# Two attentions in a fused two-layer kernel: the last heads merged without a detour, and another order of score, product and first-pass matmuls in every slot

## What is computed

```python
# layer 0 (4096 given keys) and layer 1 (1024 keys from the same tokens), per head
scores = einsum('bqhd,khd->bhqk', Q, K) * SCALE
attn = softmax(scores, axis=-1)
out = einsum('bhqk,khd->bqhd', attn, V).reshape(B, QL, HIDDEN)
x = x + gate * (out @ Wo.T)          # layer 1 adds a bias as well
```

## Time and profile before

| | us |
|---|---|
| median of three runs (2009.97 to 2014.08) | 2013.04 |
| the profiled execution's own time | 2001.37 |
| its span in the trace | 1999.5 |
| PE busy in the span | 1757.2 |
| DVE busy | 1423.7 |
| ACT busy | 1091.8 |
| POOL busy | 509.8 |

### The profile page before, as it was taken

How to read it: one execution, slowest core, us unless ns; L and a number is a source line. 1 busy time by engine, 2 the same in 40 slices (tenths; PEclk the granted TensorE clock), 3 DMA queues, 4 the chain that set the end, 5 groups by cost and what they waited for, 6 DMA issues and landing times. The chain is left out here.

```text
span 1999.5 us, 28186 instructions
## 1 busy us (share of the span) xinstructions
PE 1757.2 (88%) x9884; PEld 1042.1 (52%) x9884; DVE 1423.7 (71%) x1910; ACT 1091.8 (55%) x2169; POOL 509.8 (25%) x524
## 2 busy tenths in 40 slices
PE   4699999999999999467998664999999999769997
PEld 3233333333333333343343223888888888658885
DVE  4589999999999994565897536666666666556666
ACT  0178888888888885233786412545455445324342
POOL 4333344333454500031213202111011110012223
PEclk8689999999999999676998856999999999879998
DMA  3202111113111100202444101000000000023331
GB/s 121 57 27 59 40 40 50 53 44 95 44 53 52 54 20 24 75 16 44 99 99 132 63 26 33 22 9 21 21 13 21 10 19 3 9 75 110 114 116 59
DMA packets 50127, 102.18 MB, mean 51 GB/s; under 512 B 10279, under 2 KB 20471, under 8 KB 48497
## 3 DMA queue, kind: packets, MB, share of 16 engines
q1 hardware_dynamic: 49745, 100.47, 18.0%
q10 hardware_dynamic: 288, 0.49, 0.2%
HBM read 68.19 MB, written 17.01 MB: 43 GB/s over the span
## 5 line engine op out<-in xcount | busy, mean ns | idle before, releaser
L660 DVE TENSOR_REDUCE a_max_part<-psum 128x1 f32<-128x1024 f32 x640 | 752.6, 1218 | 111.6 <-PE psum L549 109.9
L730 ACT ACTIVATE a_probs<-psum 128x512 f32<-128x512 f32 x1280 | 671.3, 601 | 187.5 <-PE psum L600 186.7
L600 PE MATMUL psum<-a_q_max,a_k_rows 51*128 51x512 f32 x1280 | 467.7, 457 | 7.8 <-ACT a_probs L730 6.0
L600 PEld LDWEIGHTS psum<-a_q_max,a_k_rows 51*128 51x128 f32 x1280 | 214.5, 191 | 369.8 <-ACT a_probs L730 297.3
L549 PE MATMUL psum<-a_k_rows,a_q_rows 48*128 48x512 f32 x1280 | 366.1, 485 | 31.5 <-DVE a_max_part L660 12.4
L589 PE MATMUL psum<-a_probs,a_v_ext 128*32 128x512 f32 x2560 | 353.6, 623 | 1.5 <-ACT a_probs L730 1.5
L549 PEld LDWEIGHTS psum<-a_k_rows,a_q_rows 48*128 48x128 f32 x1280 | 158.4, 194 | 110.3 <-DVE a_max_part L660 85.2
L1687 PE MATMUL psum<-high_t_parts,high_gu 128*128 128x512 f32 x600 | 146.5, 394 | 6.8 <-DVE high_t_parts L1781 6.8
L359 POOL TENSOR_TENSOR a_k_rows<-a_k_in,a_k_rows 16x2048 fp32r<-16x2048 f32 x32 | 146.9, 4592 | 2.5
L483 POOL TENSOR_TENSOR a_max_bf<-a_neg_max,a_zeros 128x8 bf16<-128x8 f32 x64 | 14.5, 227 | 470.7 <-issue 408.2
L1392 PE MATMUL psum<-wide_k_t,wide_q_t 128*128 128x512 f32 (+3 forms) x576 | 130.8, 353 | 1.7 <-DVE wide_id_bf L1591 1.7
(11 more groups left out here) (193 smaller groups left out, 2059.7 us busy)
## 6 DMA issues: line engine op xcount, KB each, us to landing
o<-a_o_out SPq DMA_DIRECT2D x60, 256.0 KB, 2.0
a_k_in<-in_k SPq DMA_DIRECT2D x32, 256.0 KB
a_q_rows<-q_high SPq DMA_DIRECT2D x124, 64.0 KB, 2.4
gu_in<-in_w_gu SPq DMA_DIRECT2D x25, 256.0 KB, 2.9
high_cw<-cw SPq DMA_DIRECT2D x24, 256.0 KB, 3.8
a_k_in<-in_k SPq DMA_DIRECT2D x32, 128.0 KB
a_v_in<-in_v SPq DMA_DIRECT2D x16, 256.0 KB, 12.8
a_o<-o SPq DMA_DIRECT2D x8, 512.0 KB
```

The source lines that it names most:

```text
L600: pe.matmul(psum[:, self.bank_of(self.filling(j)), :], k_rows[rows, b, k0:k0 + P], self.q_max[rows, u % 2, :], start=True, stop=True).then ...
L660: dve.tensor_reduce(self.max_part[:, u % 2, c // self.nch, c % self.nch:c % self.nch + 1], psum[:, 2 * (n % 2):2 * (n % 2) + 2, :], AX.XY, ...
L730: act.activation(self.probs[:, p % self.pring, :], psum[:, self.bank_of(self.filling(j)), :], ACT.Exp).then_inc(self.exp_done, 1)
```

## The change

- **Slot order** (both attentions): two second scores, a pair of first scores, (the turning of maxima), one second score, the products with values, one second score, a pair of first scores.
- **Direct heads.** Heads 14 and 15 both stay on the core (`o_out` has four buffers). A token tile of 128 is one product of `o_out` with `w_direct`: the weights repeated for the four strips, with a column that adds up the denominators. DVE then takes a reciprocal per token and one `scalar_tensor_tensor` adds to x. There are 16 such steps, and four pair steps for the merged heads 0 to 13: 20 in all (`product`, `add_out`). 16 of them lie behind the last ten slots in the first attention, 10 behind the last five in the second (`steps_after`); the others follow the last product with values.
- **Merged heads** have two parts, 0 to 7 and 8 to 13; the second is loaded in two portions. Loads, additions, reciprocals and scaling move to other units, one addition of sums per unit in place of two; the last additions are on POOL, none on DVE.
- **The gate** is multiplied into the weights on POOL (`gate_weights`, unit 11), and the bias's steps come two units later.
- **The first loads of q** of three heads are shared between SP's and ACT's queues.

```diff
-LAST = H - 1
...
-    PARTS = ((0, 8, 0, 0), (8, 12, 1, 0), (12, LAST, 1, 64))
+
+
+    PARTS = ((0, 8, 0), (8, DIRECT[0], 1))
+    STEPS = 20
+    PAIRS = 12
...
+    def load_direct(self, sp, g):
+        if g == 0:
+            sp.wait_ge(self.w_clear, 1)
+        sp.dma_start(self.w_direct[32 * g:32 * g + HD, :, 0:D],
+                     self.w_dram[HD * DIRECT[0]:HD * H, :].rearrange("(h d) n -> d h n", d=HD)).then_inc(self.w_loaded, 16)
...
+    def widen(self, sp, n):
+        lo, hi, c = self.PARTS[n]
+        sp.wait_ge(self.rec_stored[n], 16)
+        if n > 0:
+            sp.wait_ge(self.o_ready[n - 1], 1)
+        sp.dma_start(self.rec_wide[self.rows(n), :],
+                     self.den_dram[lo:hi, :].unsqueeze(1).broadcast_to([hi - lo, HD, T])).then_inc(self.wide_loaded[n], 16)
...
+    def gate_weights(self, pool):
+        gate = self.gate.unsqueeze(1).broadcast_to([P, 2, D])
+        pool.wait_ge(self.w_loaded, 80)
+        pool.tensor_tensor(self.w[:, :, :], self.w[:, :, :], gate, ALU.mult).then_inc(self.w_gated, 1)
+        pool.tensor_tensor(self.w_direct[:, :, 0:D], self.w_direct[:, :, 0:D], gate, ALU.mult).then_inc(self.w_gated, 1)
+        pool.wait_ge(self.w_gated, 2)
...
+    def is_pair(self, k):
+        return self.PAIRS <= k < self.PAIRS + 4
+
+    def tile_of(self, k):
+        return k if k < 8 else k - 8 if k < self.PAIRS else k - self.PAIRS
...
-    def scale_last(self, dve, half):
-        dve.wait_ge(self.last_full, half + 1)
-        for i in range(2):
-            cut, out = slice(256 * i, 256 * (i + 1)), slice(QH * half + 256 * i, QH * half + 256 * (i + 1))
-            dve.reciprocal(self.rec_last[:, cut], self.psum[0:HD, 2, cut]).then_inc(self.rec_last_ready, 1)
-            dve.wait_ge(self.rec_last_ready, 2 * half + i + 1)
-            dve.tensor_tensor(self.o_last[:, out], self.psum[0:HD, 3, cut], self.rec_last[:, cut], ALU.mult).then_inc(self.last_done, 1)
...
+        if self.is_pair(k):
+            i = k - self.PAIRS
+            dve.wait_ge(self.out_free, 8 + 2 * i + 2 if i < 2 else 2 * i + 2)
+            dve.tensor_tensor(self.x[:, 2 * i:2 * i + 2, :], self.x[:, 2 * i:2 * i + 2, :],
+                              self.psum[:, bank, :].rearrange("p (a n) -> p a n", n=D), ALU.add).then_inc(self.out_free, 1)
+            return
+        t = self.tile_of(k)
+        dve.reciprocal(self.rec_token[:, k:k + 1], self.psum[:, bank, D:D + 1]).then_inc(self.token_ready, 1)
+        dve.wait_ge(self.token_ready, k + 1 - (4 if k >= self.PAIRS else 0))
+        if k >= 8:
+            dve.wait_ge(self.out_free, t + 1 if k < self.PAIRS else self.PAIRS + t // 2 + 1)
+        dve.scalar_tensor_tensor(self.x[:, t, :], self.psum[:, bank, 0:D], self.rec_token[:, k:k + 1], self.x[:, t, :],
+                                 ALU.mult, ALU.add).then_inc(self.out_free, 1)
...
-    def select_last(self, pe, half):
-        pe.wait_ge(self.o_full, 2 * LAST + half + 1)
...
+        if k >= 4:
+            pe.wait_ge(self.out_free, k - 3)
+        if self.is_pair(k):
+            i = k - self.PAIRS
+            if i == 0:
+                for ready in self.o_ready:
+                    pe.wait_ge(ready, 1)
+            deep = self.rows(1)
+            for a in range(2):
+                token, out = slice((2 * i + a) * P, (2 * i + a + 1) * P), self.psum[:, bank, a * D:(a + 1) * D]
+                pe.matmul(out, self.o[:, 0, token], self.w[:, 0, :], start=(a == 0), stop=False)
+                mm = pe.matmul(out, self.o[deep, 1, token], self.w[deep, 1, :], start=False, stop=(a == 1))
+            mm.then_inc(self.out_full, 1)
+            return
+        t, n = self.tile_of(k), int(k >= 8)
+        pe.wait_ge(self.o_full, 2 * DIRECT[n] + t // 4 + 1)
+        pe.matmul(self.psum[:, bank, 0:D + 1], self.o_out[:, 2 * n + t // 4, (t % 4) * P:(t % 4 + 1) * P], self.w_direct[:, n, :],
+                  start=True, stop=True).then_inc(self.out_full, 1)
...
+    def steps_after(self, u, g):
+        if self.groups >= 8:
+            s = (u - 2 * DIRECT[1]) * self.groups + g - 6
+            if 0 <= s < 6:
+                return range(2 * s, 2 * s + 2)
+            return range(s + 6, s + 7) if 6 <= s < 10 else range(0)
+        s = (u - 2 * DIRECT[1]) * self.groups + g + 1
+        return range(2 * s, 2 * s + 2) if 0 <= s < 5 else range(0)
...
@@ -428,9 +465,8 @@
             sp.wait_ge(self.q_set, 1)
             if not raw:
                 sp.wait_ge(self.k_set, 1)
-            load_q(sp, (0,), q_rows[:, 0, :], k_rows[:, 0, :], 0, self.q_loaded[0])
-            for h in range(1, first_heads):
-                load_q(sp, (0, 1), q_rows[:, h, :], k_rows[:, h, :], h, self.q_loaded[h])
+            for h in range(first_heads):
+                load_q(sp, (0,), q_rows[:, h, :], k_rows[:, h, :], h, self.q_loaded[h])
             got = first_heads
             if raw:
                 sp.wait_ge(self.v_ready, 1)
...
@@ -456,16 +492,23 @@
                     sent += 1
                 if u == 2:
                     merge.load_weights(sp)
+                if 2 <= u < 6:
+                    merge.load_direct(sp, u - 2)
                 if u == 16:
-                    merge.load(sp, 0)
-                if u == 20:
+                    merge.load_den(sp, 0, 0, 8)
+                if u in (18, 20):
+                    merge.load_sums(sp, 0, 0, 8, range(u - 18, u - 16))
+                if u == 23:
+                    merge.store_reciprocals(sp, 0)
+                if u == 24:
                     merge.widen(sp, 0)
-                if u == 24:
-                    merge.load(sp, 1)
-                if u == 27:
-                    merge.widen(sp, 1)
-            merge.load(sp, 2)
-            merge.widen(sp, 2)
+                    merge.load_den(sp, 1, 8, 12)
+                if u == 25:
+                    merge.load_sums(sp, 1, 8, 12, range(4))
+            merge.load_den(sp, 1, 12, 14)
+            merge.load_sums(sp, 1, 12, 14, range(4))
+            merge.store_reciprocals(sp, 1)
+            merge.widen(sp, 1)
         @block.gpsimd
         def _(pool):
...
@@ -507,26 +551,22 @@
                     if raw:
                         self.split_keys(pool, h)
                 done = heads_split(u)
-                if u == 4 and merge.bias is not None:
+                if u == 6 and merge.bias is not None:
                     merge.scale_bias(pool)
-                if u in (6, 7) and merge.bias is not None:
-                    merge.add_bias(pool, u - 6)
-                if u == 18:
+                if u in (8, 9) and merge.bias is not None:
+                    merge.add_bias(pool, u - 8)
+                if u == 11:
+                    merge.gate_weights(pool)
+                if u == 21:
                     merge.add_den(pool, 0)
-                if u == 20:
-                    merge.add_sums(pool, 0, (1, 2))
-                if u == 21:
-                    merge.add_sums(pool, 0, (3,))
-                if u == 23:
+                if 22 <= u < 25:
+                    merge.add_sums(pool, 0, (u - 21,))
+                if u == 26:
                     merge.scale(pool, 0)
-                if u == 25:
+                if u == 29:
                     merge.add_den(pool, 1)
-                if u == 26:
-                    merge.add_sums(pool, 1, (1, 2))
-                if u == 27:
-                    merge.add_sums(pool, 1, (3,))
-                if u == 29:
-                    merge.scale(pool, 1)
+            merge.add_sums(pool, 1, (1, 2, 3))
+            merge.scale(pool, 1)
         @block.tensor
         def _(pe):
...
@@ -605,27 +645,27 @@
                 j = group * g
                 one = u * steps + 2 * g + ahead
                 two = one + 1
-                second_wait(u, j)
-                second_chunk(u, j)
+                for n in (j, j + 1):
+                    second_wait(u, n)
+                    second_chunk(u, n)
                 if one < self.chunks:
                     first_wait(one)
                     first_half(one, 1)
                     first_half(one, 0).then_inc(self.s1_full, 1)
-                second_wait(u, j + 1)
-                second_chunk(u, j + 1)
                 if j + 2 == self.turn_at and u + 1 < us:
                     turn_maxima(u + 1)
+                second_wait(u, j + 2)
+                second_chunk(u, j + 2)
+                if g > 0:
+                    pv_group(u, g - 1)
+                elif u > 0:
+                    pv_group(u - 1, groups - 1)
+                second_wait(u, j + 3)
+                second_chunk(u, j + 3)
                 if two < self.chunks:
                     first_wait(two)
                     first_half(two, 0)
                     first_half(two, 1).then_inc(self.s1_full, 1)
-                for n in (j + 2, j + 3):
-                    second_wait(u, n)
-                    second_chunk(u, n)
-                if g > 0:
-                    pv_group(u, g - 1)
-                elif u > 0:
```

(88 more changed lines are left out.)

118 lines of the change are left out of this document (46 added, 72 removed).

## The result

The changed kernel takes 2060.3 us in the median of four runs (2055.9 to 2062.5), the kernel before 2011.5 (2004.5 to 2014.1): a ratio of 1.0245, with a 95% interval of 1.0214 to 1.0277. The forecast was 2031.5, range 2005 to 2070. The sign was right; the size was 49 us where +18.5 was forecast. The profiled execution has a span of 2060.6 us, against 1999.5. These spans are 61 us apart and the medians only 49, as the profiled execution of the kernel before was 10 us under its median and that of the changed kernel 2 above.

What follows compares the result with a forecast made beforehand. It took the loop through ACT's exponential and the products, 2.605 us a slot, as the bound. Units +37.5, tail -5, second attention's loop +21.9, tail -36.4, gate half a microsecond: +18.5, from 2013.0 to 2031.5 us, range 2005 to 2070.

Steps and rivals of the forecast that it cites:

- The slot's loop stays at 2.605: In plain slots, the loop through ACT's exponential and the products keeps its five terms, 2.605 us; price 0.
- the ring's wait: PE's wait for a free score bank, said to hide a fifth score round of 0.23 us per slot.
- D: Slower: a same-strip weight load can't overlap a running matmul; slots of 2.75, +37 us, 2068 in all; chance 0.04.
- E: Faster: the score ahead of the products finds its bank free; slots of 2.45, -34 us, 1998 in all; chance 0.06.
- Rival B: Faster or even: the second attention's stalls vanish and both tails end well; sum -5, 2005 to 2019 us; chance 0.12.
- The wait once a unit: Slot 1's products wait for DVE's copy: 1.03 us, second attention 1.24; with the turning, +37.5 over the first attention's units.
- t0: The end of the products in slot 0 of a unit, from which the copy's end was timed.
- The turning: The turning of maxima, once a unit, lies wholly on the path: 0.22 us in the first attention, 0.16 in the second.
- The tails: Time behind each attention's last turning of maxima: -5 us in the first attention, -36.4 in the second.
- Stalls in the second attention: Stalls in the second attention's loop, 38 us before: POOL's long waits for sums and denominators go, 11.6 us stay.
- The clock: PE's granted clock falls after long waits in the second attention: 2.2 us per fall, 8 us for three or four.
- Rival C: Much slower: PE's clock falls again and again from a 1.24 us wait every second-attention unit; 2060 to 2140 us; chance 0.12.

Runs made afterwards that it cites:

- copy-early run: The changed kernel, but DVE copies the sums out after the first chunk of a unit, not the second; PE's order untouched: 1962.4 us.
- run with three useless matmuls: The changed kernel with three unneeded repeats of the third score in slot 1 of the second attention's units, ahead of the waiting products: 2030.2 us.
- order alone: The kernel before with the changed kernel's slot order and the old merging: 2104.8 us, ratio 1.0485.
- early loads: The changed kernel with sums of heads 0 to 7 loaded in units 17 and 19, added and scaled a unit later: 2057.8 us.

## Why the forecast was too small

- **The slot's loop stays at 2.605: right.** The products of neighbouring slots in the changed kernel, by the timeline of PE:

```profile
412.78 1.07 PE L629 MATMUL psum<-a_probs,a_v_ext 128*32 128x512 f32 x8
...
415.39 1.06 PE L629 MATMUL psum<-a_probs,a_v_ext 128*32 128x512 f32 x8
...
417.98 1.07 PE L629 MATMUL psum<-a_probs,a_v_ext 128*32 128x512 f32 x8
```

  They are 2.60 apart: the fifth round hides in the ring's wait. Rivals D and E fall with it, no slot of 2.75 and none of 2.45. The Trainium skill, "TensorE: Matmul & The Clock Gate", Part 3, on which D leaned, lets a load run beside a matmul only where the row group differs. By that rule five exposed loads would stand in this slot; the trace disagrees with it here too. Rival B falls as well: it needed the stalls of the second attention to vanish, and 28 us of them are left, as shown below.
- **The wait once a unit: right.** The copy was forecast to be seen at t0 + 2.635; the load starts at t0 + 2.68. The first attention's unit is 22.58 where 22.59 followed, and the term of +37.5 measures +38.8. The copy-early run takes the wait away and leaves PE's order as it is, and the units go to 21.50.
- **The turning: right**, 0.19 and 0.17 in the copy-early run, against 0.22 and 0.16; its slot is 3.27, against 3.255.
- **The tails: right within 2 us**, -3.6 (forecast -5) and -34.7 (forecast -36.4).
- **Stalls in the second attention: too small.** 11.6 us were forecast. The run with three useless matmuls has a loop of 234.8 us, of which 29 units of 7.14 are 207; so 28 us are stalls, with the falls of the clock that they bring along: 11.9 in the one unit of 19.05 (1.9 forecast), 5.1 where POOL waits for the widened reciprocals (3.7 forecast), 4.0 in the last two units (0.3 forecast), 6.8 in the others (5.7 forecast). The step that failed is the sentence that the waits of 9 to 11 us for sums go, since "loads are issued units before POOL needs them". POOL needs all four strips' sums for its first addition. SP issues the last two in its unit 20, once DVE has copied that unit's sums, and POOL comes to its unit 22 early, as it splits the maxima of the unit after. So the two steps are 6 us apart and not two units: issued at 1154.37, awaited from 1160.37, there at 1167.03, 12.7 us after the issue. Nor are POOL's waits for DMAs gone but for one or two. There are five of 30.4 us in all, three of them in the loop (6.66, 7.31 and 5.67), where the kernel before had six of 34.4. The first row was misread as well: its 9.90 us are a wait for DVE's copy. The wait for sums stands elsewhere in that trace:

```profile
1121.40 2.33 POOL L173 TENSOR_TENSOR h_t<-a_o 64x1024 f32<-64x1024 f32 x1 [9.35 <-DMA a_o<-o]
```

- **The clock: the term that failed most.** I allowed 8 us for three or four falls. It was 30.8, the difference between the changed kernel's loop and that of the useless matmuls. A fall costs two units of 7.14 another 2.7 us (7.70 + 9.28 - 14.28); I had 2.2. The size of one was near, the number of them wrong: I tied the fall to a long wait for POOL and took the new wait of 1.24 us in every unit for harmless. The two terms were 19.6 us together and measured 58.5.
- **The sum.** The like of the profiled execution was forecast at 2019.9 and took 2062.5, 42.6 more; these two terms make 38.9 of it. One slip is in the working: with all stalls gone the loop would be 7.1 x 29 = 205.9, which is +2.3 and not +3.5; nothing but rival B's sum hangs on it. The result lies in the range of 2005 to 2070 only because the range was drawn out for C and D; the forecast's own, 2018 to 2046, missed it.
- **Rival C** named this mechanism, with the right point from which it decides, and gave 2060 to 2140; the result lies at its lower end. The fault was to give it 0.12 and to leave it out of the sum. No row of the kernel before showed a wait of about a microsecond that comes back every unit, so nothing in the trace spoke against it. In the first attention C didn't come true: the wait is 1.02 us there, but once in 22.6 us, and the granted clock is 1.00 on the mean of the 679 us; one unit of 24.2 us has a short stretch at the lower level.

What stays open: the order alone has 16 us more in the first attention than the wait explains (two long units and a longer tail) with the old merging. That part wasn't taken apart. Also open is why the second attention's loop, in the new order, is 265.6 us with the new merging and 253.5 with the old one; the early loads take those 12 us from the loop, but the tail gives back 9. And why the two orders differ at a wait of about 1 us is not known.

## What to carry to other kernels

When an edit moves a consumer ahead in one engine's order, move its producer's step on the other engine with it: here one index in DVE's order was worth 98 us. A short wait can have two prices, its own length and what it does to TensorE's clock, and here the second hung on how often it returned: 1.2 us in every 7 cost nearly as much again through the clock (30.8 us over 29 units, beside 36 for the wait itself), 1.0 in every 22.6 hardly more than itself. And of two edits that come in one change, measure each alone: the merging gave 53 us, the order hid it.

## What the hardware showed that I had not expected

More work made the kernel faster: 87 useless matmuls in 29 units took 30 us off, as the granted clock over these units rose from 0.74 to 0.92. In the new order, with 0.51 us idle ahead of the products in a unit of 7.14 no ordinary unit ran slow; with 0.98 in 7.13 some did, with 1.22 most did. In the old order, with 1.01 in 6.78 eleven in a row stayed up, with 1.37 in 7.13 most fell. And the low level held on by itself: in the old order with 1.01 us idle the granted clock was 0.50 when the loop began and stayed so for its first three units, of 10.34 each. Later it stayed low behind a stalled unit of 11.2 us, for one more of 10.34. The same program has two paces there, and its four times lie between 1987.0 and 2006.9 us.
